# Two-part operands for the head projections of a two-layer gated cross-attention and expert kernel

## The reference

```
x = x + tanh(g_xattn[0]) * _L0_xattn_ref(_layernorm(x), ctx, ...)   # returns y @ Wp + bp, y = self + cross heads
x = x + tanh(g_ffn[0])   * _L0_ffn_ref(_layernorm(x), ...)          # softmax(xf @ Ws + bs), top_k, experts
x = x + tanh(g_xattn[1]) * _L1_xattn_ref(_layernorm(x), ctx, ...)   # returns concat @ Wo + bo
x = x + tanh(g_ffn[1])   * _L1_ffn_ref(_layernorm(x), ...)
```

## Time and profile before

| | us |
|---|---|
| median of three executions | 4030.9 |
| range of the three | 4030.63 to 4036.47 |
| the profiled execution, its own time | 4039.2 |
| the profiled execution, its span from first to last instruction | 4037.5 |

### The profile page before, as it was taken

How to read it: one execution, slowest core, us unless ns; L and a number is a source line. 1 busy time by engine, 2 the same in 40 slices (tenths; PEclk the granted TensorE clock), 3 DMA queues, 4 the chain that set the end, 5 groups by cost and what they waited for, 6 DMA issues and landing times. The chain is left out here.

```text
span 4037.5 us, 76143 instructions
## 1 busy us (share of the span) xinstructions
PE 3698.3 (92%) x30244; PEld 2594.3 (64%) x30244; DVE 2506.9 (62%) x2873; ACT 2060.4 (51%) x3649; POOL 1770.6 (44%) x874
## 2 busy tenths in 40 slices
PE   6989699999999998869996699999998859999998
PEld 5768456666665664459995355555554548888886
DVE  4345687878888784666664677777773553333342
ACT  2222266666666665146662366666665144444432
POOL 0000287687778777002110488888886011111110
PEclk9999799999999999879998799999999869999999
DMA  4478724424442431636653522222211423333341
GB/s 160 166 235 296 203 77 104 109 74 105 98 114 59 110 87 45 227 118 201 219 186 115 148 78 79 75 80 78 76 44 55 174 87 117 117 117 108 115 113 38
DMA packets 290266, 485.13 MB, mean 120 GB/s; under 512 B 23104, under 2 KB 121408, under 8 KB 287936
## 3 DMA queue, kind: packets, MB, share of 16 engines
q1 hardware_dynamic: 274368, 443.01, 36.5%
q0 software_dynamic: 14080, 37.76, 4.1%
q10 hardware_dynamic: 1536, 0.40, 0.1%
HBM read 350.67 MB, written 130.02 MB: 119 GB/s over the span
## 5 line engine op out<-in xcount | busy, mean ns | idle before, releaser
L803 ACT ACTIVATE attn_probs<-attn_low 128x512 f32<-128x512 f32 (+1 forms) x2368 | 1234.6, 595 | 467.4 <-PE attn_low L714 351.7
L844 DVE TENSOR_REDUCE attn_parts<-attn_mx 128x4 f32<-128x2048 f32 x538 | 1232.8, 2291 | 366.3 <-PE attn_mx L686 365.6
L665 POOL TENSOR_TENSOR attn_psums<-attn_psums,attn_probs 128x1024 f32<-128x1024 f32 x536 | 1275.1, 2379 | 66.6 <-ACT attn_probs L803 1.4
L714 PE MATMUL attn_low<-attn_queries,attn_keys 97*128 97x256 f32 (+1 forms) x4736 | 914.7, 311 | 13.5 <-ACT attn_probs L803 5.5
L714 PEld LDWEIGHTS attn_low<-attn_queries,attn_keys 97*128 97x128 f32 x4736 | 658.3, 190 | 371.7 <-ACT attn_probs L803 187.7
L731 PE MATMUL attn_low<-attn_probs,attn_values 128*32 128x256 f32 x9472 | 629.4, 383 | 1.4 <-ACT attn_probs L803 1.4
L1528 DVE TENSOR_TENSOR ring_low<-ring_raw,ring_high 128x2048 fp32r<-128x2048 f32 x128 | 293.1, 2292 | 206.7 <-ACT ring_high L1485 206.7
L662 POOL TENSOR_TENSOR attn_psums<-attn_probs 128x1024 f32<-128x1024 f32 x88 | 209.6, 2382 | 371.6 <-ACT attn_probs L803 371.6
L731 PEld LDWEIGHTS attn_low<-attn_probs,attn_values 128*32 128x32 f32 x9472 | 247.6, 109 | 182.8 <-issue 2.1
L1442 PE MATMUL ffn_up<-ffn_xH,ring_high 128*128 128x256 f32 (+1 forms) x1024 | 351.0, 343 | 2.7 <-DVE ffn_xL L1534 2.7
L1442 PE MATMUL ffn_up<-ffn_xH,ring_low 128*128 128x256 f32 (+1 forms) x1024 | 348.2, 340 | 0.0
(11 more groups left out here) (200 smaller groups left out, 4434.6 us busy)
## 6 DMA issues: line engine op xcount, KB each, us to landing
ring_raw<-in_L_ffn_W_dram SPq DMA_DIRECT2D x128, 1024.0 KB, 5.5
attn_keys<-l_cross_keys SPq DMA_DIRECT2D x96, 512.0 KB, 6.9
attn_queries<-l_queries SPq DMA_DIRECT2D x48, 512.0 KB, 4.8
l_cross_keys<-projc_high SPq DMA_DIRECT2D x64, 256.0 KB, 2.2
l_cross_keys<-projc_lowp SPq DMA_DIRECT2D x64, 256.0 KB, 2.4
l_cross_values<-projc_vout SPq DMA_DIRECT2D x64, 256.0 KB, 2.5
attn_keysn<-l_cross_keys SPq DMA_DIRECT2D x16, 1024.0 KB, 5.0
attn_values<-l_cross_values SPq DMA_DIRECT2D x32, 512.0 KB, 8.3
```

Of the source, the lines that this page charges most:

```text
L665: pool.tensor_tensor(ps, ps, at, ALU.add).then_inc(added, 1)
L714: mm = pe.matmul(out[:, n0:], KS[b][0:3 * HD + 1, h, kb * P:(kb + 1) * P], QS[b][0:3 * HD + 1, h, job.qb * QB + n0:(job.qb + 1) * QB], sta ...
L803: act.activation(probs[:, m % RING, i // 2, heads, n0:], sc[:, item % SC, :].rearrange("p (h q) -> p h q", q=QB)[:, :, n0:], ACT.Exp, scal ...
L844: op = dve.tensor_reduce(into, seen, AX.X, ALU.max)
```

## The change

The projection `y @ W` is no longer one float32 product but three float32r products: `yH @ WH`, `yL @ WH`, `yH @ WL`, all summed in the same PSUM bank. For that

- the weights come in four transfers of 256 KB, one per 128 rows; ScalarE makes `woH` of each, VectorE makes `woL`;
- for each unit ScalarE makes `yH` from the heads' outputs; the low part `yL` is made by VectorE for units 0 and 1 (block 0) and by GpSimd for units 2, 3 and 4;
- ScalarE's split of the next block stands before `std(t)` at tiles 1, 5 and 9; `add_heads` moves on VectorE from behind tile 1, 5, 9 to behind tile 0, 4, 8;
- SyncE loads block i + 2 at tile 1 and 5, when the low parts of the block before are made (before: at tile 4 and 8, when the products or the sum of the block two before were done);
- VectorE makes, before its loop, in this order: (`add_heads(0)`), the low part of unit 0, the four low parts of the weights, (`add_heads(1)`), the low part of unit 1.

```diff
+        woH, woL = (ph.sb(f"wo{part}", [P, C, D], F32R) for part in "HL")
+        yH, yL = ([ph.sb(f"y{part}{n}", [P, C, BLK], F32R) for n in range(2)] for part in "HL")
...
+        BY_DVE = part_of[TB]
+
+        def wait_low(eng, u):
+
+            if u < BY_DVE:
+                eng.wait_ge(y_low, u + 1)
+            else:
+                eng.wait_ge(y_low_pool, u - BY_DVE + 1)
...
-                sp.dma_start(wo[:, :, :], w_out.rearrange("(c p) n -> p c n", p=P)).then_inc(wo_in, DMA)
+                for ch in range(C):
+                    sp.dma_start(wo[:, ch, :], w_out[ch * P:(ch + 1) * P, :]).then_inc(wo_in[ch], DMA)
...
-                            if both:
-                                sp.wait_ge(y_sum, part_of[(i - 2) * TB + TB - 1] + 1)
-                            else:
-                                sp.wait_ge(product, (i - 1) * TB)
-                            load_y(part_of[i * TB])
                             sp.wait_ge(summed, (i - 1) * TB)
                             load_res(i)
+                        if t % TB == 1 and t // TB + 2 < BLOCKS:
+                            wait_low(sp, part_of[t])
+                            wait_low(sp, part_of[t // TB * TB + TB - 1])
+                            load_y(part_of[(t // TB + 2) * TB])
...
                 def products(t):
-                    if t == 0:
-                        pe.wait_ge(wo_in, DMA)
-                    if both:
-                        pe.wait_ge(y_sum, part_of[t] + 1)
-                    else:
-                        pe.wait_ge(y_in[part_of[t]], DMA)
+                    wait_low(pe, part_of[t])
...
-                        mm = pe.matmul(bank[t % 4][:, :], yt[t // TB % 2][:, ch, n0:n0 + P], wo[:, ch, :],
-                                       start=ch == 0, stop=ch == C - 1)
+                        if t == 0:
+                            pe.wait_ge(wo_low, ch + 1)
+                        for n, (y, w) in enumerate(((yH, woH), (yL, woH), (yH, woL))):
+                            mm = pe.matmul(bank[t % 4][:, :], y[t // TB % 2][:, ch, n0:n0 + P], w[:, ch, :],
+                                           start=ch == 0 and n == 0, stop=ch == C - 1 and n == 2)
...
+            @block.gpsimd
+            def _(pool):
+                for u in range(BY_DVE, len(PARTS)):
+                    pool.wait_ge(y_high, u + 1)
+                    pool.tensor_tensor(cut(yL, u), cut(yt, u), cut(yH, u).bitcast(F32), ALU.subtract).then_inc(y_low_pool, 1)
...
+                def split_high(u):
+                    if both:
+                        act.wait_ge(y_sum, u + 1)
+                    else:
+                        act.wait_ge(y_in[u], DMA)
+                    if PARTS[u][0] >= 2 * BLK:
+                        act.wait_ge(product, PARTS[u][0] // P - TB)
+                    act.activation(cut(yH, u), cut(yt, u), ACT.Copy).then_inc(y_high, 1)
+
+                split_high(0)
+                for ch in range(C):
+                    act.wait_ge(wo_in[ch], DMA)
+                    act.activation(woH[:, ch, :], wo[:, ch, :], ACT.Copy).then_inc(wo_high, 1)
+                for u in range(1, BY_DVE):
+                    split_high(u)
                 for t in range(TILES + 2):
+                    if t % TB == 1 and t < TILES - TB:
+                        split_high(part_of[(t // TB + 1) * TB])
...
                     if PARTS[u][0] >= 2 * BLK:
-                        dve.wait_ge(product, PARTS[u][0] // P - TB)
+                        wait_low(dve, part_of[PARTS[u][0] // P - TB - 1])
...
+                def split_low(u):
+                    dve.wait_ge(y_high, u + 1)
+                    dve.tensor_tensor(cut(yL, u), cut(yt, u), cut(yH, u).bitcast(F32), ALU.subtract).then_inc(y_low, 1)
...
-                if both:
-                    for u in range(part_of[TB]):
+                for u in range(BY_DVE):
+                    if both:
                         add_heads(u)
+                    split_low(u)
+                    for ch in range(C) if u == 0 else ():
+                        dve.wait_ge(wo_high, ch + 1)
+                        dve.tensor_tensor(woL[:, ch, :], wo[:, ch, :], woH[:, ch, :].bitcast(F32), ALU.subtract
+                                          ).then_inc(wo_low, 1)
...
-                        if both and t % TB == 1 and t < TILES - TB:
+                        if both and t % TB == 0 and t < TILES - TB:
                             add_heads(part_of[(t // TB + 1) * TB])
```

More of the change, by code:

```diff
@@ L906, in out_stage @@
         lg = ph.ps("lg", (P, TILES, E))
-        (wo_in, bo_in, wr_in, y_sum, product, bank_read, summed, stats_ready, var_ready, std_ready, rstd_ready, xn_ready,
+        (wo_high, wo_low, y_high, y_low, y_low_pool, bo_in, wr_in, y_sum, product, bank_read, summed, stats_ready, var_ready, std_ready, rstd_ready, xn_ready,
          turned, xT_ready, routed, copied, cleared) = (
-            ph.sem(x) for x in ("wo_in", "bo_in", "wr_in", "y_sum", "product", "bank_read", "summed", "stats_ready",
+            ph.sem(x) for x in ("wo_high", "wo_low", "y_high", "y_low", "y_low_pool", "bo_in", "wr_in", "y_sum", "product", "bank_read", "summed", "stats_ready",
                                 "var_ready", "std_ready", "rstd_ready", "xn_ready", "turned", "xT_ready", "routed",
                                 "copied", "cleared"))
+        wo_in = [ph.sem(f"wo_in{ch}") for ch in range(C)]
         y_in = [ph.sem(f"y_in{u}") for u in range(len(PARTS))]
```

## The result

| | before | after |
|---|---|---|
| median, measured side by side (16 executions each), us | 4033.4 | 4041.2 |
| ratio to before, 95% interval | | 1.0016 [1.0008, 1.0023] |
| the profiled execution, its own time, us | 4039.2 | 4042.3 |
| its span, us | 4037.5 | 4040.7 |
| mean granted TensorE clock | 0.953 | 0.949 |

The changed kernel is slower by 0.16%, about 6.5 us by the ratio; the medians lie 7.8 us apart. The prediction had 4.1 us faster, 4026.8, and its range ended at 4035. It started from 4030.9, a median of three executions; over sixteen the kernel before has 4033.4, so 2.5 of the 14.4 us between forecast and measured time are the starting point. Both intervals hold a loss of 0.08% to 0.14%, 3 to 6 us.

The account below looks back on a forecast made before the run. TensorE was taken to set the pace, 4.77 us a tile. `out1` gaining 6.3 us and `out0` losing 2.2 made 4.1 faster: 4026.8 from a median of 4030.9, range 4013 to 4035, chance 0.55.

Parts of the forecast that it names:

- The products: Each tile of both stages: products to turns 3.51 to 2.89 us, period 4.77 to 4.15, 6.8 saved over eleven periods.
- The 18% by the trace's rows: Product time saved by twelve float32r products at 0.234 us each; the skill's four-pass count would save a quarter.
- GpSimd's duration: Low part of 128x2048 on GpSimd, extrapolated from two smaller sizes: 4.57 us.
- the rival with 7 us: GpSimd's low part takes 7.0 us under the lock, making the kernel 10.5 us slower, 4041.4; chance 0.10.
- The lock: GpSimd's low part bars VectorE's `residual`, `add_heads` and `normalize` for its whole instruction, up to 4.57 us.
- the rival without it: GpSimd's low part never delays VectorE; together 14.4 us faster, 4016.5; chance 0.28.
- What it costs in the middle of a stage: Blocks 2 and 3, TensorE standing on late `xT`: 1.6 us in `out1`, 3.9 in `out0` with `add_heads`.
- The starts without the lock: Start of `products(4)` against before, if GpSimd bars nothing: 2.0 us behind in `out0`, 3.4 ahead in `out1`.
- The load in `out0`: `add_heads` of block 1 waits for its transfer; TensorE stands 3.5 us, `products(4)` start 4.5 behind with the lock.
- the clock: After the 3.5 us of standing in `out0`, products(3) and (4) may run cold: 1.2 us, between 0 and 2.3.
- the start of `out1`: Up to `products(4)`, with GpSimd's low part of block 1 delaying `normalize(1)`: 0.5 us ahead of before.
- the others keep ahead of TensorE: Start of `out1`: after the first weight's low part, those of the other weight parts never make products wait.

Follow-up runs that it names:

- e3: Changed kernel with each of GpSimd's 128x2048 low-part instructions cut into four of 128x512; ratio 0.9996 to the kernel before.
- e4: Kernel before, with GpSimd subtracting unused 128x2048 tiles of its own once per tile from tile 4 in both stages; ratio 1.0170 to the kernel before.
- e1: Changed kernel without GpSimd's low part of blocks 1 to 3, the same twelve products a tile, result incomplete; ratio 0.9971 to the kernel before.
- e5: Changed kernel with idle products filling three places where TensorE stands in the first block; ratio 0.9992 to the kernel before.
- e7: Changed kernel with the weights in one 1 MB transfer instead of four; ratio 1.0005 to the kernel before.
- e8: Changed kernel with ScalarE's copy `xT(t - 2)` put ahead of `std(t)`; ratio 0.9975 to the kernel before.
- e9: Changed kernel with all low parts on VectorE and ScalarE's copy `xT(t - 2)` ahead of `std(t)`; 4017.7 us, ratio 0.9961 to the kernel before.

## Why the prediction was wrong

**What held.** *The products*: 2.86 us from products to turns (2.89 forecast) and 4.10 a tile (4.15). Over the eleven periods that is 7.3 us gained a stage where 6.8 were forecast. The 18% by the trace's rows stood, and not a quarter: 3.51 to 2.86 is 18.5%. The four passes that the Trainium skill (FP8 and Floating Point Precision, section TensorE Precision Notes) counts for true float32 fit the rows before, sixteen in 3.51 us, 0.22 each; it is the twelve float32r products, 0.24 each in 2.86 us, that take more than a pass. *GpSimd's duration*: 4.57 forecast, 4.57 to 4.60 measured where it was let in at once; the rival with 7 us is out, and that its 4041.4 lies beside the measured 4041.2 is chance. *The lock*: `normalize`, `residual` and nothing that reads PSUM, for the whole instruction, so the rival without it is out as well. The Trainium skill (SBUF — State Buffer, section "SBUF: two separate sides") has one port pair that is held for the whole instruction, against VectorE operations with two inputs there or in a two-port mode, and e3, e4 and the changed kernel agree: 0.54 became 3.11 and 3.45, and up to 4.30. *What it costs in the middle of a stage*, `add_heads` included: 1.6 forecast in `out1`, 1.4 measured; 3.9 in `out0`, 3.5 measured. *The starts without the lock*: 2.0 behind and 3.4 ahead forecast, 1.7 behind and 2.9 ahead in e1. *The load in `out0`*: `add_heads` waited 2.71 us for block 1, and `products(4)` came 5.2 us late, for 4.5 forecast.

**What failed: the clock.** The sum had 1.2 us for it, once, in `out0`, taken between 0 and 2.3 "neither end being nearer". Measured against 4.08 a tile it was 2.8 (tile 4) and 1.6 (tile 12) in `out0` and 1.9 (tile 4) in `out1`; beside these the scores of tile 0, at the lower level, took 1.43 and 1.85 us instead of 0.96, another 1.4. That is 7.7 in place of 1.2, 6.5 us more, about the whole difference of 6.1 between forecast and measured stages. e5 changed nothing but TensorE's standing and took 5.3 us back, with 1.6 of half clock left in the middle of `out0`. The term was priced as one event of one tile, though the same text had TensorE stand in `out1` and behind each block as well.

**What failed: the start of `out1`.** `products(4)` were to be 0.5 us ahead and were 1.7 behind, 2.2 short. The chain behind the lock was right, but GpSimd began 18.0 us into the stage, not 16.5, since ScalarE's split of block 1 started 1.5 us later than forecast, 15.95 us in, when its load had landed:

```profile
3126.76 0.77 PE L990 MATMUL out_bank<-out_woH,out_yH 128*128 128x512 f32 x1 [13.38 <-DVE out_woL L1114]
3127.13 1.96 ACT L1039 ACTIVATE out_woH<-out_wo 128x512 fp32r<-128x512 f32 x3 [1.94 <-DMA out_wo<-in_L_xattn_Wo_dram]
...
3133.43 0.75 DVE L1083 SCALAR_TENSOR_TENSOR out_xnew<-out_tmp,keep_tanhg,out_xres 128x512 f32<-128x512 f32 x1 [0.71 <-DMA out_xres<-x]
...
3135.17 0.30 ACT L1049 ACTIVATE out_std<-out_mv,keep_eps 128x1 f32<-128x1 f32 x1 [3.00 <-DVE out_mv L1091]
...
3135.96 1.92 ACT L1034 ACTIVATE out_yH<-out_yin 128x2048 fp32r<-128x2048 f32 x1 [0.50 <-DMA out_yin<-l_y]
...
3137.96 4.56 POOL L1023 TENSOR_TENSOR out_yL<-out_yin,out_yH 128x2048 fp32r<-128x2048 f32 x1 [21.30 <-ACT out_yH L1034]
...
3139.36 3.45 DVE L1102 TENSOR_SCALAR out_xn<-out_xnew,out_mv,out_rstd 128x512 f32<-128x512 f32 x1
...
3142.86 0.66 PE L999 MATMUL out_turn<-keep_ident,out_xn 128*128 128x128 f32 x4 [2.38 <-DVE out_xn L1102]
...
3145.37 1.85 PE L1007 MATMUL out_lg<-out_wr,out_xT 128*128 128x8 f32 x8 [1.85 <-ACT out_xT L1055]
```

The load was issued 3.9 us into the stage, behind three more issues for the weights, where it was 2.6 before. The prediction gave this lateness at most 1.5 us in `out0` and forgot it in `out1`. It also left out that the split stands on ScalarE behind `std(0)`, which ended only 0.5 us before the load landed, since `residual(0)` had waited 0.71 us for the residual input. An earlier load alone would have gained those 0.5 us, no more; in e7, with a later first product, `std(0)` was as late as the block had been. A smaller miss is "the others keep ahead of TensorE": the second part of the weights landed 2.9 us after the first here (3124.26 and 3127.11), and ScalarE was idle 1.94 us for it; in the second trace of the changed kernel it was 0.6 us. The other 0.7 us of the 2.2 are about what the scores lost at the lower clock (0.9), counted above already.

**The sum again.** Start: 0.7 and 2.2 us worse than forecast. Eleven periods: 2.1 and 1.1 worse (the clock 3.2 and 1.9, less what lock and period turned out better). Tail: 0.4 worse, 0.3 better. Together 6.1 to 6.2 with the rounding. The medians say 7.8 and 3.0 us slower, the stages 2.0 and 2.3. In the first pair 4.7 us of the gap lie in which executions were profiled: that of the kernel before took 5.8 us more than its median, that of the changed kernel 1.1. Why the executions differ so stays open.

**The range.** It ended at 4035, 8 above the forecast. A text whose whole argument is that TensorE stands in new places, and which notes that it worked at half clock after standing, should have let every such place cost a cold tile: six blocks at its own 2.3 us are 14 us where the sum had 1.2, and the upper end would have stood near 4040; at the 2.8 us measured in tile 4 it would be 4042.

## What to carry to other kernels

Before work is given to GpSimd because it is idle, look for VectorE's two-input and fast one-input operations on on-chip memory beside it: here each could be late by one whole GpSimd instruction, so either cut that in pieces no longer than the slack, or leave it on VectorE. Follow the delay to TensorE through every list written out by hand: here the order of two operations on ScalarE decided between 186.8 and 168.7 us. And where TensorE will stand in a place where it did not stand before, let the range reach to a tile at half clock for each place: here it was 1.6 to 2.8 us at three of them, and nothing at the others.

## What the runs showed of the hardware

The shutting out goes both ways. Where `residual` was already under way, GpSimd's instruction was the one to wait, 4.91 us instead of 4.56:

```profile
3157.14 0.75 DVE L1083 SCALAR_TENSOR_TENSOR out_xnew<-out_tmp,keep_tanhg,out_xres 128x512 f32<-128x512 f32 x1
3157.44 4.91 POOL L1023 TENSOR_TENSOR out_yL<-out_yin,out_yH 128x2048 fp32r<-128x2048 f32 x1 [14.92 <-ACT out_yH L1034]
```

Four pieces of 128x512 on GpSimd took 5.8 us where one of 128x2048 took 4.57, 1.2 us more in all; a part of that is pieces that waited for VectorE in their turn (up to 1.75 us, beside 1.26 at the least).

The granted clock did not follow the length of a wait in a simple way. In `out0` of the changed kernel it fell after 2.98, 2.36 and 1.85 us of standing within 11, and once after 1.47 us alone, some 2 us after TensorE had begun again (1678.0 to 1680.0); it didn't fall after 1.30 us in the same stage. In e8 it fell right after 3.58 us of standing, over tile 3. But in e9 it stayed at 1.00 through waits of 2.93 and 1.49 us, and in e1 through 2.47 and 1.86. Which standing brings it down was not settled.
